# Second attention on one Trainium2 core: four tiles in flight, stacked queries and keys through memory

## What is computed

```python
q = (x @ Wq.T).reshape(B, S, NUM_HEADS, HEAD_DIM).transpose(0, 2, 1, 3)
k = (x @ Wk.T)...      # the same shape; v = x @ Wv.T
q, k = q * cos + rotate_half(q) * sin, k * cos + rotate_half(k) * sin
scores = q @ k.T / sqrt(HEAD_DIM)      # only keys of the window, up to the token itself
out = softmax(scores) @ v              # heads side by side, then out @ Wo.T
```

## Time and profile before

| | us |
|---|---|
| median of 3 runs | 897.98 (896.47 to 900.95) |
| profiled execution | 895.71 |
| its span, first to last instruction | 893.7 |
| TensorE busy | 712.6 (80%), mean granted clock 0.853 |
| VectorE, ScalarE, GpSimd busy | 461.0, 265.0, 140.9 |
| second attention, first row scores of tile 0 to last weighing | 323.5 to 665.6 |

### The profile page before, as it was taken

The page is one execution under the profiler, slowest core; times in us unless marked ns, Lnnn a source line. Parts: engine busy times, 40 slices in busy tenths (PEclk is TensorE's granted clock), DMA queues, the critical chain, the costliest instruction groups (busy, mean ns, idle before and its releaser), DMA issues.

```text
span 893.7 us, 19827 instructions
## 1 busy us (share of the span) xinstructions
PE 712.6 (80%) x8484; PEld 575.5 (64%) x8484; DVE 461.0 (52%) x1206; ACT 265.0 (30%) x430; POOL 140.9 (16%) x205
## 2 busy tenths in 40 slices
PE   4976669856689848688888889898677999888985
PEld 3765557645577637577777767676554777667762
DVE  3446555284677853654555556564545623222345
ACT  4110010300135334343435343534353112222223
POOL 2000000000001100213131222313140431111153
PEclk9996559975589978595989989897779999999998
DMA  8090000000040020000000000000020476999646
GB/s 288 18 371 4 4 39 1 1 3 4 5 163 26 1 80 0 1 0 3 1 2 1 1 1 1 1 1 1 1 72 1 151 308 243 345 350 354 216 141 188
DMA packets 28791, 75.79 MB, mean 85 GB/s; under 512 B 4704, under 2 KB 6368, under 8 KB 28704
## 3 DMA queue, kind: packets, MB, share of 16 engines
q1 hardware_dynamic: 23664, 58.01, 18.3%
q0 software_dynamic: 5040, 16.52, 5.2%
HBM read 51.97 MB, written 22.54 MB: 83 GB/s over the span
## 4 chain that ended last, share of the span: by engine, by line
PE 56%; DVE 14%; issue 9%; ACT 8%; DMA 8%; POOL 4%; SPq 1%; POOLq 0%; ACTq 0%; DVEq 0%
PE bank L363 26%; PE bank L585 7%; ACT FP L1220 6%; DMA FP<-slots_in 6%; PE bank L571 5%; PE bank L507 4%; PE bank L423 3%; PE bank L433 3%; PE bank L374 2%; PE bank L561 2%; DVE FP L856 2%; DVE FP L765 2%; POOL slots_in L1419 2%; POOL FP L1429 2%; DVE kraw L1035 2%
## 5 line engine op out<-in xcount | busy, mean ns | idle before, releaser
L1220 ACT ACTIVATE FP<-bank 128x512 f32<-128x512 f32 (+1 forms) x218 | 118.5, 585 | 256.7 <-PE bank L363 132.7
L363 PE MATMUL bank<-W,XR 128*128 128x512 f32 x672 | 164.2, 401 | 9.6 <-DVE W L765 4.8
L363 PEld LDWEIGHTS bank<-W,XR 128*128 128x128 f32 x672 | 127.2, 193 | 37.6 <-DVE W L765 5.2
L1035 DVE CUSTOM_DVE_ANT_0 kraw<-bank,maskb 128x256 bf16<-128x256 f32 (+1 forms) x256 | 89.1, 404 | 85.5 <-PE bank L561 85.5
L363 PE MATMUL bank<-FP 128*128 128x128 f32 x558 | 88.6, 314 | 0.8 <-ACT FP L1220 0.8
L571 PE MATMUL bank<-RP 64*128 64x128 f32 x480 | 50.7, 340 | 38.8 <-ACT FP L1220 38.8
L1408 POOL TENSOR_SCALAR_AFFINE_SELECT FP<-FP 128x512 f32<-128x512 f32 x64 | 41.6, 674 | 252.4 <-ACT FP L1220 252.4
L1220 ACT ACTIVATE FP<-FP 128x512 f32<-128x512 f32 (+2 forms) x33 | 27.2, 825 | 181.0 <-DVE FP L765 181.0
L571 PEld LDWEIGHTS bank<-RP 64*128 64x128 f32 x480 | 42.2, 240 | 52.3 <-ACT FP L1220 45.7
L363 PEld LDWEIGHTS bank<-FP 128*128 128x128 f32 x558 | 66.3, 195 | 2.8 <-DVE FP L765 1.6
L1220 ACT ACTIVATE RP<-bank 128x512 fp32r<-128x512 f32 x72 | 40.5, 596 | 88.1 <-PE bank L507 75.4
(11 more groups left out here) (125 smaller groups left out, 923.8 us busy)
## 6 DMA issues: line engine op xcount, KB each, us to landing
FP<-in_experts_dram SPq DMA_DIRECT2D x31, 768.0 KB, 5.7
FP<-slots_in SPq DMA_DIRECT2D x31, 256.0 KB, 6.4
slots_out<-FP POOLq DMA_DIRECT2D x31, 256.0 KB, 6.0
slots_in<-RP SPq DMA_DIRECT2D x7, 1024.0 KB, 10.8
FP<-in_shared_dram SPq DMA_DIRECT2D x4, 768.0 KB, 4.3
X<-in_x_dram SPq DMA_DIRECT2D x2, 1024.0 KB, 6.5
out_dram<-X SPq DMA_DIRECT2D x8, 256.0 KB, 2.8
FP<-in_bias_dram SPq DMA_DIRECT2D x2, 768.0 KB, 6.6
```

The source lines that it names most:

```text
L363: mm = nc.tensor.matmul(bank, lhs, rhs, start=(n == 0), stop=(n == len(terms) - 1))
L1035: ins = nc.vector.tensor_tensor_reduce(masked[:, 2 * (f % 2) + m, 0:n], b[:, m, :], maskb[:, m0:m0 + n], 1.0, -BIG, ALU.add, ALU.max, hmax ...
L1220: return nc.scalar.activation(o, i, func, **kw)
```

## The change

**Steps.** The pairs of `between` and score loop go. One loop runs on each engine over i = -1 to 7 and eight steps s. In it four tiles are in flight: t = i + 2 is projected and stacked, r = i + 1 has its row scores, i its key scores, exponentials, masks and weighings, d = i - 1 its division and output. Each step has one round of row scores and one of key scores and a piece of the rest.

**Stacking.** The rotated queries or keys of a tile are turned once without being stacked (4 turns each into one A bank), ScalarE writes the high part from there and VectorE the low part to `parts`, SyncE writes these three times as 256 KB to a region of DRAM (`ys`, which the experts use later), so that the three row groups of each head interleave there, and GpSimd's queue reads 48 rows for each half, 8 KB each, twice, to `qS` (three buffers) or `kS` (four). The maxima are turned too, in two halves of 16 heads (`turn_maxima`), and GpSimd's queue moves them from `mxT` to two rows of `qS`. Scores use 48 or 50 rows instead of 64. The -1 rows of `kS` are set once by four GpSimd clears.

**Also moved.** V holds row scores only; all else of these steps goes through A. `context_out` goes from VectorE to ScalarE, the high part of turned x and context too. `weigh` takes four column positions in turn instead of two, and writes 17 rows for each head instead of 32. The relay stands in SyncE's queue ahead of the shared experts' weights. The roots of tiles 0 to 6 stand behind the last copy of the context. The block of SyncE's program now stands behind TensorE's in the file. The core of the diff:

```diff
+        qS = [t.rearrange("p (a q) -> p a q", q=P) for t in (XR[:, 2048:4096], QS[:, 0:2048], QS[:, 2048:4096])]
+        kS = RP[:, :].rearrange("p (s a k) -> p s a k", s=4, k=P)
+        parts = QS[:, 5120:6144].rearrange("p (a n) -> p a n", a=2)
+        vaug = FP[:, 6144:8320].rearrange("p (s h r) -> p s h r", s=4, r=HD + 1)
+        PT = [FP[:, a:a + 1024].rearrange("p (w h q) -> p w h q", w=2, h=G) for a in (8320, 9344, 10368, 11392)]
+        mxT = QS[0:H, 17472:17728].rearrange("p (f q) -> p f q", q=P)
+        mx = FP[:, 17728:17760].rearrange("p (a l r) -> p a l r", a=2, l=2)
...
+        relay_in = [ys[a:a + 3 * P, :].bitcast(F32R).rearrange("(d m) n -> d (m n)", m=4) for a in (3 * P, 0)]
+        relay = [ys[a:a + 3 * P, :].rearrange("(x b m) n -> b x m n", b=3, m=4) for a in (3 * P, 0)]
...
+            def turn_rotated(t, n):
+                pe.wait_ge(rotated, 2 * t + 2 - n)
+                b = A.fill(pe, ("turned", t, n))
+                for c in range(DC):
+                    mm = nc.tensor.transpose(b[:, c * P:(c + 1) * P], rowf[:, c * P:(c + 1) * P], ident[:, :])
+                mm.then_inc(A.full, 1)
+            def turn_maxima(t, f):
+                pe.wait_ge(max_ready, 2 * t + f + 1)
+                b = A.fill(pe, ("mx", t, f))
+                nc.tensor.transpose(b[0:H, 0:P], mx.rearrange("p a l r -> p (a l r)"), ident[:, :]).then_inc(A.full, 1)
...
+            project2(0, 1)
+            project2(0, 2)
+            turn_rotated(0, 1)
+            project2(0, 0)
+            turn_rotated(0, 0)
+            turn_x(1)
+            pe.wait_ge(ones_ready, 1)
+            for i in range(-1, T):
+                t, r, d = i + 2, i + 1, i - 1
+                for s in range(8):
+                    if s == 0 and t < T:
+                        project2(t, 1)
+                    if r < T:
+                        row_scores(r, s)
+                    if i >= 0 and (s % 2 == 0 or i >= 1):
+                        key_scores(i, 2 * (s // 2), s % 2)
+                    if s == 1 and i >= 0:
+                        turn_maxima(i, 1)
+                    if s == 1 and d >= 0:
+                        context_rows(A, d)
+                    if s == 2 and t < T:
+                        turn_rotated(t, 1)
+                        project2(t, 0)
+                    if s == 3 and d >= 0:
+                        turn_context(A, d)
+                    if s == 4 and t < T:
+                        turn_rotated(t, 0)
+                    if s == 5 and r < T:
+                        turn_maxima(r, 0)
+                    if s == 5 and t < T:
+                        project2(t, 2)
+                    if s == 6 and d >= 0:
+                        output(A, d)
+                    if s == 7 and t + 1 < T:
+                        turn_x(t + 1)
+                    if i >= 0 and s in (3, 5, 7):
+                        weigh(i, s // 2 - 1)
...
+            def relay_rows(t, n):
+                m = 2 * t + 1 - n
+                if t >= 1:
+                    sp.wait_ge(stack_in[n], 32 * t)
+                for blk, l in ((0, 0), (1 + n, 0), (2 - n, 1)):
+                    if l == 0:
+                        sp.wait_ge(parts_high, m + 1)
+                    else:
+                        A.drained(sp, ("turned", t, n))
+                    sp.dma_start(relay[n][blk], parts[:, l, :].bitcast(F32)).then_inc(parts_out, 16)
+            for t in range(T):
+                relay_rows(t, 1)
+                relay_rows(t, 0)
...
+            def rotate(t, n):
+                name = ("qkv", t, n)
+                if n == 1 and t >= 1:
+                    A.filled(v, ("turned", t - 1, 0))
+                elif n == 0:
+                    A.filled(v, ("turned", t, 1))
+                if (t, n) == (0, 1):
+                    v.wait_ge(w_split, 6)
+                else:
+                    v.wait_ge(rotated, 2 * t + 1 - n)
+                b = A.take(v, name)[:, :].rearrange("p (h d) -> p h d", d=HD)
+                o = rh.rearrange("p (h d) -> p h d", d=HD)
...
+                tt(rowf.rearrange("p (c x m) -> p c m x", c=4, m=4), rh.rearrange("p (c m x) -> p c m x", c=4, m=4),
+                   rt.rearrange("p (c m x) -> p c m x", c=4, m=4), ALU.add).then_inc(rotated, 1)
+            def parts_low(t, n):
+                b = A.take(v, ("turned", t, n))
+                v.wait_ge(parts_high, 2 * t + 2 - n)
+                if t == 0 and n == 1:
+                    A.drained(v, ("qkv", 0, 2))
+                tt(parts[:, 1, :], b[:, :], parts[:, 0, :].bitcast(F32), ALU.subtract).then_inc(A.free, 1)
...
+            def maxima_split(i, f):
+                V.drained(v, ("rowscores", i, 8 * f + 7))
+                m = hmax[:, 16 * f:16 * f + 16].rearrange("p (r a) -> p a r", a=2)
+                own(nc.vector.tensor_copy(mx[:, :, 0, :].bitcast(F32R), m))
+                tt(mx[:, :, 1, :], m, mx[:, :, 0, :], ALU.subtract).then_inc(max_ready, 1)
+            def maxima_out(i, f):
+                b = A.take(v, ("mx", i, f))
+                if i >= 1:
+                    v.wait_ge(max_in[f], 32 * i)
+                nc.vector.tensor_copy(mxT[:, f, :], b[0:H, 0:P]).then_inc(A.free, 1)
...
+            rotate(0, 1)
+            parts_low(0, 1)
+            rotate(0, 0)
+            parts_low(0, 0)
+            low_dense(("x2", 1), xa[1], xa[0])
+            for i in range(-1, T):
+                t, r, d = i + 2, i + 1, i - 1
+                for s in range(8):
+                    if s == 0 and t < T:
+                        rotate(t, 1)
+                    if r < T:
+                        row_maxima(r, s)
+                    if s == 1 and i >= 0:
+                        maxima_out(i, 1)
+                    if s == 1 and d >= 0:
+                        context_divided(A, d)
+                    if s == 2 and t < T:
+                        parts_low(t, 1)
+                        rotate(t, 0)
+                    if s == 3 and r < T:
+                        maxima_split(r, 0)
+                    if s == 3 and d >= 0:
+                        low_dense(("co", d), ca[1], ca[0])
+                    if s == 4 and t < T:
+                        parts_low(t, 0)
+                    if s == 5 and r < T:
+                        maxima_out(r, 0)
+                    if s == 6 and d >= 0:
+                        add_output(A, d)
+                    if s == 7 and r < T:
+                        maxima_split(r, 1)
+                    if s == 7 and t + 1 < T:
+                        if i < 1:
+                            A.drained(v, ("qkv", t, 2))
+                        low_dense(("x2", t + 1), xa[1], xa[0])
+                if i == T - 2:
+                    shared_low(0)
+                    shared_low(1)
             normalise(slice(0, T - 1), 4)
...
+            shared_low(2)
...
+            def parts_out_high(t, n):
+                b = A.filled(s, ("turned", t, n))
+                m = 2 * t + 1 - n
+                if m >= 1:
+                    s.wait_ge(parts_out, 48 * m)
+                act(parts[:, 0, :], b[:, :], ACT.Copy).then_inc(parts_high, 1)
+            def values_out(t, before):
+                A.drained(s, before)
+                b = A.take(s, ("qkv", t, 2))
+                act(vaug[:, t % 4, :, 0:HD], b[:, :].rearrange("p (h d) -> p h d", d=HD), ACT.Copy).then_inc(A.free, 1)
+            def high_dense(name, hi):
+                b = A.filled(s, name)[:, :].rearrange("p (c n) -> p c n", c=DC)
+                act(hi, b, ACT.Copy).then_inc(xt_high, 1)
+            def context_out(i, a):
+                s.wait_ge(weighed, 8 * i + 4 * a + 4)
+                if i >= 1:
+                    A.filled(s, ("context2", i - 1, a))
+                act(cT[:, a * 512:(a + 1) * 512], C.banks[a][:, :], ACT.Copy).then_inc(ctx_ready, 1)
...
+            context_out(T - 1, 1)
+            roots(slice(0, T - 1), 4)
...
+            for n in range(4):
+                nc.gpsimd.memset(kS[:, n].bitcast(F32), -1.0).then_inc(minus_ready, 1)
+                if n == 0:
+                    p.wait_ge(w_split, 4)
+                    nc.gpsimd.memset(vaug[:, :, :, HD:HD + 1], 1.0).then_inc(ones_ready, 1)
...
+            def stack_rows(t, n):
+                p.wait_ge(parts_out, 48 * (2 * t + 2 - n))
+                if t >= 3:
+                    S.filled(p, ("keyscores", t - 3, 7, 1 if t >= 4 else 0))
+                if n == 1:
+                    p.wait_ge(minus_ready, min(t, 3) + 1)
+                rows = relay_in[n]
+                for a in range(2):
+                    dst = (qS[t % 3], kS[:, t % 4])[n][KS * a:KS * a + 3 * HD]
+                    nc.gpsimd.dma_start(dst.rearrange("d a q -> d (a q)"), rows[3 * HD * a:3 * HD * a + 3 * HD]).then_inc(stack_in[n], 16)
+            def stack_maxima(t, f):
+                A.drained(p, ("mx", t, f))
+                for a in range(2):
+                    place = KS * a + 3 * HD
```

(17 more changed lines are left out.)

541 lines of the change are left out of this document (220 added, 321 removed).

## The result

| | before | after |
|---|---|---|
| median, us, 20 runs each | 898.52 (891.15 to 905.40) | 893.89 (886.13 to 899.30) |
| ratio, 95% interval | | 0.9929 (0.9907 to 0.9952) |
| profiled execution, and its span | 895.71, 893.7 | 896.0, 894.1 |
| TensorE busy, mean granted clock | 712.6, 0.853 | 690.3, 0.820 |
| first row scores of tile 0 | 323.48 | 344.32 |

The change does what it says, and the time is outside of my range (822 to 872). The two profiled executions don't differ by the 4.6 us of the medians, so where those few us arise can't be read from them. What they show is why nearly fifty are missing. One execution of the study, the profiled one of experiment 1, lies over 1.5% above the fastest of its kernel and is left out of its median and ratio.

What follows compares the result with a forecast made beforehand. Bound: TensorE in one half of a tile, its exchange with ScalarE in the other. Last weighing 590.0 at full clock, plus 20 for clock, is 610, 55.6 earlier; tail +8.0, credit 2: from 895.7 to 846 us, range 822 to 872.

Steps and rivals of the forecast that it cites:

- credit for a cheaper weighing: Sum of the forecast: two TensorE holes that a faster weighing would close give back 2 us.
- What bounds the kernel: Second attention before: TensorE bounds one half of a tile, its S-bank exchange with ScalarE the other, about 1 us waited per round.
- The steady tile: Middle tiles after the change: 33.65 us between key projections at full clock, work 28.8 and holes 4.9; clock taken as 0.90.
- the rival of 0.77: Granted clock 0.77 throughout: 14 us more in the tiles, 5 at the ends, 865 us; chance 0.13.
- Start: Before tile 0's row scores: GpSimd work stretches VectorE's rotation addition, ending at 316; scores start at 333, 9.5 us late.
- Tiles 0 and 1: First rounds at full clock: 21.4 us to the end of tile 0's key projection round, then 27.7, reaching 382.1.
- Ends: Last two iterations: 22.9 us without a projection, then 19.5, paced by the S exchange and products; last weighing at 590.0.
- My 3.3 us to spare: Steady tile: the queries' stack lands at P+30.3 and is first wanted at P+33.65, P being step 0's key projection end.
- Tail: After the last weighing: roots and normalisation of tiles 0 to 6 stand ahead of the last division, adding 8.0 us.
- Transfers: Rival: stacks take 10 us instead of 4.9 and set the pace in start and tiles, 870 us; chance 0.10.
- the first rival: Cheaper weighing, each 0.5 to 0.7 us less, and clock near 1.0; VectorE's chain lets little through: 826 us; chance 0.22.
- the overlap might not come off: In-order two-bank rings make engines wait for each other; period stays at 40 us, 878 us in all; chance 0.06.

Runs made afterwards that it cites:

- experiment 1: Changed kernel with three GpSimd clears moved ahead of the stretch before tile 0, the fourth and the product of W behind the first two stacks: 884.74 us, 0.9811.
- experiment 12: Kernel before the change, with three added matmuls (result overwritten) ahead of seven of eight key scores of tiles 1 to 6: 893.06 us, 0.9897.
- experiment 5: Changed kernel with 12, 7 and 4 added matmuls (result overwritten) per tile, where TensorE waited at steps 0, 3 and 4: 869.39 us, 0.9689.
- experiment 9: Changed kernel with GpSimd clears and tail work moved earlier, added matmuls in each tile's three holes and in the last two iterations: 856.11 us, 0.9487.
- experiment 2: Changed kernel, last iteration only: tile 6's output and addition at step 4, roots of tiles 0 to 6 behind step 5: 889.64 us, 0.9895.

## Why the prediction was wrong, step by step

The traces let the miss be split: 896.0 measured in the profiled execution, 846 predicted. (Row scores of iteration 6 were to start at 382.1 + 168.3 - 2.8 = 547.6 at full clock.)

| stretch | predicted, with its share of clock | measured | miss |
|---|---|---|---|
| row scores of tile 0 start | 333 | 344.3 | 11.3 |
| to the second key projection's end | 49.1 + 5 | 64.3 | 10.2 |
| to row scores of iteration 6 | 165.5 + 11 | 192.6 | 16.1 |
| to the last weighing | 42.4 + 4 | 53.7 | 7.3 |
| tail (10.6 of earliness, 0.6 left) | 8.0 | 10.0 | 2.0 |
| credit for a cheaper weighing | -2 | 0 | 2.0 |
| experts, from the exponential to the end | 0 | 0.9 | 0.9 |

**What bounds the kernel: right in the main.** Before, the exchange with ScalarE paces the rounds of the score half that have no weighing in front (1.98 us, also at full clock in experiment 12). But TensorE does not wait ahead of each of the eight rounds, as I had read: in the tile at 464.35 it waits ahead of five, and behind a weighing not at all.
**The steady tile: right in length, and the clock is the step that failed.** Period 33.65 followed, 33.73 at a clock of 1.00 (experiment 5). That the length came out to 0.1 us is luck in part, for its two terms were off against each other: 32.07 of TensorE's time with 6.1 of fillers (3.02, 1.88, 1.18) is 26.0 of work, not 28.8, the weighings being 1.07 each, which leaves 7.7 for holes where I had 4.9. That the cheaper work didn't shorten the tile bears out the remark that VectorE's chain would let little through. "I take 0.90 in steady tiles (the holes of 2.7 and 0.6 lie close together, as before)" is the sentence that is wrong. Before, the waits were 1 us each with matmuls between; after, one is 3.2 us, and 0.81 was granted. The slope was about right: 38.47 us at 0.81 against 33.73 at 1.00 is 25 us per unit, and I had scaled to 22. Had the rival of 0.77 been taken for the forecast, it would have given 865, still 29 too low, since it left the start alone.
**Start: the mechanism was named, but put on the wrong instruction.** I let GpSimd stretch only the addition of the rotation and set its end at 316. It was the normalisation ahead of it that stood still, with the low part of W and the rotation queued behind (end 322.0), 6 us; TensorE, idle for 12.57, then ran its projections slowly (5.01 and 4.60, mean clock 0.69 from 306 to 344 us). So the keys' relay had landed at 328.0, 5.7 later than I had it, the queries' at 337.4, 9.9 later, since VectorE had to wait 3.39 for the slow query projection ahead of their rotation; and their stack took 6.9 where I had 5.5. Over all tiles the way through memory was sized well: relay 2.8 us and stack 5.6 in the median, where I had 3.7 and 4.9.
**Tiles 0 and 1** had 49.1; with fillers in the holes and a clock of 0.91 they still took 27 and 36 us (experiment 9), 62.9 in all. So with most of the clock given back they are hardly shorter. Part is the filler itself (4.99 us in a hole of some 3), part waits for tile 1's and 2's query stack: 3.21 and 1.18 us there, 1.22 at 409.86 in the changed kernel. I had said there would be none but at the very start; for the first tiles nothing covers the relay. How the rest of the 13.8 us splits is open.
**Ends.** 53.7 at 0.66. They begin with a wait that I had excluded: the row scores of iteration 6 (601.25) stand idle for 2.19, and in `row_scores` what step 0 asks for is the stacks. The queries' stack was issued at 594.30, and such transfers landed after 4.5 to 6.7 us. My 3.3 us to spare lie under the next key projection, and iteration 6 has none. It wasn't settled how much the clock alone costs there, since the fillers of experiment 9 cost what they gave.
**Tail: right** in mechanism, 8.0 against 10.0, but not in the place. Up to the second half of the last division it lost 6.3 us (8.5 behind the last weighing, where the kernel before took 2.1). The other 3.7 came behind the division, where the clock was 0.78 from 655 to 693 us and had been 1.00: turns and products of TensorE took 1.94, 1.09, 3.96 and 4.50 us, before the change 1.25, 0.63, 3.00 and 2.94. In experiment 2 only the 4.50 is left of these, and there that stretch is 1.6 longer than before the change.
**Rivals.** Transfers do not pace the steady tiles. Of the waits from 300 to 680 us (in total, times, longest), which answer to the earlier trace rows, GpSimd's three for the keys' relays end at 328, 354 and 388.5 (two for the queries' at 337.5 and 364.5), while TensorE's for L1053 come in every tile:

```profile
PE bank L500 <- DVE hmax L1053: 45.6, 28, 3.2
...
POOL RP L1480 <- DMA slots_out<-QS: 32.3, 3, 15.8
```

The cheaper weighing of the first rival came, its full clock did not. That the overlap might not come off (878) was nearest in number, but for the wrong reason: with the clock given back, the overlap is there.
The spread of my range was too small because I let the clock vary by 0.13 and the start by its transfers alone, and treated them as independent of the hole that I had myself put into every tile.

## What to carry to other kernels

When a reordering makes the matrix engine wait in one piece, price the hole twice: its own length, and the work behind it at half clock. Here waits of 3.2, and of 1.7 and 0.9 us, made two products of 3.0 us take up to 5.1 and 5.3. Count that before counting saved instructions, and test it with fillers in the hole and beside it; only if the first gains and the second loses is it the clock. And where a second engine clears or copies while VectorE has a chain of SBUF work, look at every instruction of the chain, not only at those with two inputs.

## What the runs showed of the hardware that I had not expected

- TensorE with 23 more matmuls of 128x512 in each tile finished 24 us earlier (869.4 against 893.9). Of twelve more the place alone decides: 882.5 in the hole, 910.9 behind the output product. The Trainium skill ("TensorE: Matmul & The Clock Gate", A second HAM failure mode: psum-queue depth-cycling) describes a bf16 kernel whose clock swings because TensorE idles briefly between groups of matmuls as it goes round PSUM banks; the trace agrees, with waits of 3.21 and 1.71 us for two V banks and products of 5.05 and 5.31 us behind them.
- GpSimd's clears, which read nothing, held up a VectorE operation with one SBUF input: 5.39 us for one normalisation of 128x512, where four take 1.92. Beside another clear an addition with two SBUF inputs kept its 1.07.
- Stepping through four column positions, 32 records of 128x17 by 128 columns took 1.07 us, 33 ns each; by position 2.41 us, 75 ns each.
- The last addition of the rotation took 1.07 to 1.08 us with its strided output in the changed kernel, also with GpSimd at rest; with plain output it was 0.69.
